# Vision block, prologue and early steps re-ordered, late query/key products in two banks

## The reference

```python
x = layernorm(patches, ln1_g, ln1_b)              # 768 wide
x = layernorm(x @ W + bias, ln2_g, ln2_b) + pe     # 256 wide
h = concat(cls_token + cls_pos, x)                 # 37 tokens
h = h + attention(layernorm(h))                    # 16 heads of 16, rotary on q and k
h = h + ffn(layernorm(h))                          # 256-1024-256, ternary weights, 8-bit tokens
```

## Time and profile before

| | us |
|---|---|
| median of 3 runs | 382.64 (382.4 to 383.99) |
| the profiled execution, its own time | 384.33 |
| its span, first to last instruction | 382.5 |
| TensorE busy | 324.6 |
| VectorE busy | 280.2 |
| ScalarE busy | 217.6 |
| GpSimd busy | 163.5 |

### The profile page before, as it was taken

One profiled execution on the slowest core, in us unless ns is written; L12 is line 12 of the kernel. 1 busy time (PEld: TensorE's weight loads), 2 busy tenths in 40 slices (PEclk: granted clock), 3 DMA queues, 4 the chain that ended last, 5 costly groups with the idle time before them and its releaser, 6 DMA issues.

```text
span 382.5 us, 9772 instructions
## 1 busy us (share of the span) xinstructions
PE 324.6 (85%) x3540; PEld 253.6 (66%) x3548; DVE 280.2 (73%) x683; ACT 217.6 (57%) x395; POOL 163.5 (43%) x330
## 2 busy tenths in 40 slices
PE   1868889999999676899898989889887798999874
PEld 1657777777764332798787878788775476777553
DVE  3599766776856436268967677776766999999983
ACT  2356556575443211435455554646453799999993
POOL 2276534655535436244523233232204456556630
PEclk9999999999999999559999999999999999999997
DMA  8996600000000000000000000000000001000101
GB/s 237 354 402 190 215 3 0 1 2 0 0 3 0 0 0 2 2 2 3 2 1 0 0 0 0 0 0 0 0 2 0 1 2 39 32 27 30 44 28 62
DMA packets 9018, 16.10 MB, mean 42 GB/s; under 512 B 944, under 2 KB 5744, under 8 KB 8992
## 3 DMA queue, kind: packets, MB, share of 16 engines
q1 hardware_dynamic: 7936, 13.59, 10.4%
q10 hardware_dynamic: 1056, 2.18, 1.8%
HBM read 13.34 MB, written 2.42 MB: 41 GB/s over the span
## 4 chain that ended last, share of the span: by engine, by line
PE 49%; DVE 19%; ACT 13%; issue 12%; POOL 4%; DMA 3%; ACTq 0%; DVEq 0%; POOLq 0%
PE ps L333 11%; PE ps L426 10%; DVE sc L837 6%; PE ps L363 5%; DVE ximg L856 4%; PE ps L458 4%; POOL qr L1091 3%; PE ps L434 3%; PE ps L323 3%; ACT ximg L1049 3%; DMA qkT<-in_W 3%; PE ps L445 2%; ACT ximg L1002 2%; PE ps L420 2%; ACT ximg L1044 2%
## 5 line engine op out<-in xcount | busy, mean ns | idle before, releaser
L1083 POOL TENSOR_TENSOR rs<-rs,nhalf 128x1 f32<-128x1 f32 (+1 forms) x76 | 41.2, 548 | 104.9 <-DVE rs L831 43.5
L988 ACT ACTIVATE ximg<-ps,byp 128x222 f32<-128x222 f32 x64 | 25.0, 442 | 61.0 <-PE ps L466 54.1
L333 PE MATMUL ps<-w_in,xT 128*128 128x256 f32 (+1 forms) x228 | 53.2, 383 | 3.8 <-ACT xT L922 3.8
L1133 POOL TENSOR_TENSOR ximg<-qkT,ones_c 128x148 f32<-128x148 f32 x32 | 17.9, 558 | 77.8 <-PE ps L420 76.6
L426 PE MATMUL ps<-hnT,w_v 128*128 (+1 forms) x256 | 38.9, 300 | 12.8 <-ACT ximg L1002 7.6
L333 PEld LDWEIGHTS ps<-w_in,xT 128*128 128x128 f32 (+1 forms) x228 | 41.3, 187 | 11.3 <-ACT xT L922 5.6
L426 PEld LDWEIGHTS ps<-hnT,w_v 128*128 128x128 f32 x256 | 34.2, 208 | 18.2 <-issue 17.0
L363 PE MATMUL ps<-w_qk,hnT 128*128 128x512 f32 (+1 forms) x76 | 36.5, 602 | 8.0 <-DVE qb L701 8.0
L782 DVE TENSOR_TENSOR ximg<-ps,tab 111x512 f32<-111x512 f32 x32 | 22.1, 690 | 28.1 <-PE ps L445 28.1
L693 DVE TENSOR_TENSOR qa<-ps,tab 128x512 f32<-128x512 f32 (+1 forms) x19 | 13.1, 689 | 30.7 <-PE ps L316 30.7
L1091 POOL TENSOR_TENSOR qr<-qa,qb 128x512 f32<-128x512 f32 (+1 forms) x19 | 24.1, 1266 | 14.5 <-DVE qb L701 14.5
(11 more groups left out here) (108 smaller groups left out, 768.8 us busy)
## 6 DMA issues: line engine op xcount, KB each, us to landing
ximg<-in_x SPq DMA_DIRECT2D x18, 384.0 KB, 14.2
out<-ximg SPq DMA_DIRECT2D x18, 128.0 KB, 1.7
ximg<-in_W SPq DMA_DIRECT2D x2, 1024.0 KB, 6.3
...
qkT<-in_W SPq DMA_DIRECT2D x1, 384.0 KB, 4.5
qkT<-in_W ACTq DMA_DIRECT2D x1, 384.0 KB, 9.6
```

The source lines that it names most:

```text
L333: pe.matmul(dst[0:n, :], xT[t % 2][:, k, 0:n], w_in[:, k, :], start=(k == 0), stop=False)
L988: ins = act.activation(vds[u][:, m, :, :].rearrange("p i (r t) -> p i r t", r=3), src, ACT.Identity, bias=b_v[:, m:m + 1])
L1083: pool.tensor_tensor(rs[u][0:n, i:i + 1], rs[u][0:n, i:i + 1], nhalf[0:n, :], ALU.pow).then_inc(S[done], 1)
```

## The change

- **Loads.** W's two halves get semaphores of their own; the first now follows x tile 0 with nothing of the offset table among the next loads of its queue. The constant table is loaded in two parts, columns up to the position table first, then the position table behind W. The offset table is loaded in two column parts: the four that patches need on ScalarE's queue, 111 rows, the three for q, k and output on SP, behind x tile 2. `wide` is loaded in two parts, 256 columns first. x tile 3 now goes ahead of Wqk.
- **Prologue.** 14 matmuls on a block of ones before TensorE's first wait. ScalarE scales W's second half, VectorE the first, and VectorE does so before tile 1's statistics. The five operations on the offset table are re-ordered. `pixels_out(1)` goes ahead of the second bf16 part. `turn_pixels(2)` goes ahead of the offsets of tiles 0 and 1. The work on the 768 columns moves behind ScalarE's steps 3 and 5 and VectorE's steps 4 and 6.
- **`hot` in pieces** of four images, one ahead of each GpSimd step from 2 to 16; each patch offset from tile 2 on waits for its piece.
- **Steps 3 to 8** on TensorE become `early_step`: turn, product, positions, turn of h.
- **From tile 11 on**, odd query/key products go into bank 7, even ones into bank 5, and each waits for the rotation two tiles back, no longer one.

```diff
+        def qk_bank(t):
+            return 7 if t > NT - LAG + 1 and t % 2 else 5
...
             load_x(0)
-            sp.dma_start(w_raw[:, 0:3, :], w_rows[:, 0:3, :]).then_inc(S["ld_w"], 16)
+            sp.dma_start(w_raw[:, 0:3, :], w_rows[:, 0:3, :]).then_inc(S["ld_w0"], 16)
             load_x(1)
-            sp.dma_start(offs[0:48, :], spread_row(a["offsets"], 7 * D, 48)).then_inc(S["ld_offs"], 16)
             load_x(2)
+            sp.dma_start(offs[:, 4 * D:7 * D], spread_row(a["offsets"][4 * D:7 * D], 3 * D, 128)).then_inc(S["ld_rows"], 16)
+            load_x(3)
             sp.dma_start(w_qk[:], a["Wqk"].rearrange("(k p) n -> p k n", p=128)).then_inc(S["ld_qk"], 16)
-            for t in range(3, NT + 1):
+            for t in range(4, NT + 1):
...
-                if t == 2:
-                    pe.wait_ge(S["hot_done"], 2)
+                if isinstance(t, int) and t >= 2:
+                    pe.wait_ge(S["hot_done"], min(t, 16))
...
             def qk_product(t):
                 pe.wait_ge(S["h_canvas"], t + 1)
-                war(pe, "qk_rot", t, 1)
+                late = t > NT - LAG + 1
+                war(pe, "qk_rot", t, 2 if late else 1)
...
+                if qk_bank(t) == 7:
+                    pe.wait_ge(S["y_mid"], NT)
...
+            def early_step(s):
+                turn_pixels(s)
+                patch_product(s - 1)
+                position_rows(s - 2)
+                turn_h(s - 3)
...
+            pe.wait_ge(S["cset"], 1)
+            for i in range(14):
+                pe.matmul(ps[:, 7, 0:128], onesf[:, :], onesf[:, :], start=True, stop=True)
             pe.wait_ge(S["ld_tab"], 16)
             turn_pixels(0)
             patch_offset()
             patch_product(0)
             turn_pixels(1)
             patch_product(1)
+            turn_pixels(2)
             pe.wait_ge(S["hot_done"], 1)
             pe.wait_ge(S["b_done"], 1)
             product_offset(0)
             product_offset(1)
             position_rows(0)
-            turn_pixels(2)
-            for s in range(3, NT + LAG + 1):
+            for s in range(3, LAG):
+                early_step(s)
+            for s in range(LAG, NT + LAG + 1):
                 patch_step(s)
...
+            pixel_stats(0)
+            pixel_mean(0)
+            pixel_var(0)
+            v.wait_ge(S["ld_w0"], 16)
             v.wait_ge(S["ld_byp"], 16)
-            for k in range(3, KP):
+            for k in range(3):
                 ins = v.tensor_scalar(w_in[:, k, :], w_raw[:, k, :], g1[:, k:k + 1], None, ALU.mult)
             ins.then_inc(S["wg_done"], 1)
-            pixel_stats(2)
+            pixel_stats(1)
+            pixel_mean(1)
+            pixel_var(1)
...
-            patch_step(2)
-            v.wait_ge(S["b_mid"], 2)
-            leave_out(pos_rows[:, qo], bmid[0:K3, qo], 1, bres[0:K3, qo]).then_inc(S["b_done"], 1)
-            for s in range(3, NT + LAG + 1):
+            for s in range(2, NT + LAG + 1):
                 patch_step(s)
+                if s == 4:
+                    v.wait_ge(S["b_hi"], 2)
+                    leave_out(bres[0:K3, qo], bhi[0:K3, qo], 0, qko).then_inc(S["b_res"], 1)
+                if s == 6:
+                    v.wait_ge(S["b_mid"], 2)
+                    leave_out(pos_rows[:, qo], bmid[0:K3, qo], 1, bres[0:K3, qo]).then_inc(S["b_done"], 1)
...
             v.memset(ps[:, 0:4, :], 1.0)
+            v.wait_ge(S["qk_rot"], NT)
             v.memset(ps[:, 7, :], 1.0)
...
-            act.dma_start(tab[:, 0:FTAB], a["table"][:, 0:FTAB]).then_inc(S["ld_tab"], 16)
-            act.dma_start(w_raw[:, 3:6, :], a["W"].rearrange("(k p) n -> p k n", p=128)[:, 3:6, :]).then_inc(S["ld_w"], 16)
-            act.dma_start(offs[48:112, :], spread_row(a["offsets"], 7 * D, 64)).then_inc(S["ld_offs"], 16)
-            act.dma_start(wide[:, :], spread_row(a["rows"], 2 * D + F)).then_inc(S["ld_wide"], 16)
+            act.dma_start(tab[:, 0:pe_o], a["table"][:, 0:pe_o]).then_inc(S["ld_tab"], 16)
+            act.dma_start(w_raw[:, 3:6, :], a["W"].rearrange("(k p) n -> p k n", p=128)[:, 3:6, :]).then_inc(S["ld_w1"], 16)
+            act.dma_start(tab[:, pe_o:FTAB], a["table"][:, pe_o:FTAB]).then_inc(S["ld_pe"], 16)
+            act.dma_start(offs[0:K3, 0:4 * D], spread_row(a["offsets"][0:4 * D], 4 * D, K3)).then_inc(S["ld_offs"], 16)
+            act.dma_start(wide[:, 0:D], spread_row(a["rows"][0:D], D)).then_inc(S["ld_g2"], 16)
             act.dma_start(tab[:, FTAB:NTAB], a["table"][:, FTAB:NTAB]).then_inc(S["ld_rot"], 16)
+            act.dma_start(wide[:, D:2 * D + F], spread_row(a["rows"][D:2 * D + F], D + F)).then_inc(S["ld_wide"], 16)
...
+            pixels_out(1)
             act.wait_ge(S["b_res"], 1)
             act.activation(bmid[0:K3, py], bres[0:K3, py], ACT.Copy).then_inc(S["b_mid"], 1)
-            pixels_out(1)
-            act.activation(bhi[0:K3, qo], qko, ACT.Copy).then_inc(S["b_hi"], 1)
             pixels_normal(2)
-            act.wait_ge(S["b_res"], 2)
-            act.activation(bmid[0:K3, qo], bres[0:K3, qo], ACT.Copy).then_inc(S["b_mid"], 1)
             pixels_out(2)
             for s in range(3, NT + LAG + 3):
                 patch_step(s)
+                if s == 3:
+                    act.wait_ge(S["ld_rows"], 16)
+                    act.activation(bhi[0:K3, qo], qko, ACT.Copy).then_inc(S["b_hi"], 1)
+                if s == 5:
+                    act.wait_ge(S["b_res"], 2)
+                    act.activation(bmid[0:K3, qo], bres[0:K3, qo], ACT.Copy).then_inc(S["b_mid"], 1)
...
-            hot_columns(7, B)
             for s in range(2, NT + LAG + 1):
+                if s <= 16:
+                    hot_columns(4 * s - 1, min(B, 4 * s + 3))
                 patch_step(s)
```

More of the change, by code:

```diff
@@ L181, in vit_block @@
         names = (
-            "apart ld_tab ld_rot ld_w ld_byp ld_offs ld_wide ld_qk ld_v ld_o ld_f1 ld_f2 "
+            "apart ld_tab ld_pe ld_rot ld_w0 ld_w1 ld_byp ld_offs ld_rows ld_g2 ld_wide ld_qk ld_v ld_o ld_f1 ld_f2 "
             "cset crow bmix b_hi b_res b_mid b_done wg_done hot_done "
@@ L246, in vit_block, with ps_qk @@
         ps_hT = ps[:, 4, 0:D].rearrange("p (k c) -> p k c", k=2)
-        ps_qk = ps[:, 5, :]
+        def qk_bank(t):
+            return 7 if t > NT - LAG + 1 and t % 2 else 5
+        def ps_qk(t):
+            return ps[:, qk_bank(t), :]
         ps_qkT = ps[:, 6, :].rearrange("p (k c) -> p k c", k=4)
@@ L305, in patch_offset @@
             def patch_offset():
-                pe.wait_ge(S["ld_w"], 32)
+                pe.wait_ge(S["ld_w0"], 16)
+                pe.wait_ge(S["ld_w1"], 16)
                 pe.wait_ge(S["ld_byp"], 16)
@@ L360, in qk_product @@
                     pe.wait_ge(S["b_done"], 2)
-                n = rows(t)
+                if qk_bank(t) == 7:
+                    pe.wait_ge(S["y_mid"], NT)
+                n, dst = rows(t), ps_qk(t)
                 for k in range(2):
-                    pe.matmul(ps_qk[0:n, :], hnT[:, k, 128 * t:128 * t + n], w_qk[:, k, :], start=(k == 0), stop=False)
-                add_rows(ps_qk[0:n, :], t, QK_ROWS).then_inc(S["qk_ready"], 1)
+                    pe.matmul(dst[0:n, :], hnT[:, k, 128 * t:128 * t + n], w_qk[:, k, :], start=(k == 0), stop=False)
+                add_rows(dst[0:n, :], t, QK_ROWS).then_inc(S["qk_ready"], 1)
             def turn_qk(t):
@@ L568, in _ @@
         def _(v):
-            v.memset(onesf[:, :], 1.0)
+            v.memset(onesf[:, :], 1.0).then_inc(S["cset"], 1)
+            v.memset(nhalf[:, :], -0.5).then_inc(S["cset"], 1)
             v.memset(ones_c[:, :], 1.0)
@@ L652, in _ @@
             qo, py = slice(2 * D, 5 * D), slice(0, 2 * D)
-            for t in range(2):
-                pixel_stats(t)
-                pixel_mean(t)
-                pixel_var(t)
-            v.wait_ge(S["ld_w"], 32)
+            pixel_stats(0)
+            pixel_mean(0)
+            pixel_var(0)
+            v.wait_ge(S["ld_w0"], 16)
             v.wait_ge(S["ld_byp"], 16)
-            for k in range(3, KP):
+            for k in range(3):
                 ins = v.tensor_scalar(w_in[:, k, :], w_raw[:, k, :], g1[:, k:k + 1], None, ALU.mult)
             ins.then_inc(S["wg_done"], 1)
-            pixel_stats(2)
+            pixel_stats(1)
+            pixel_mean(1)
+            pixel_var(1)
             v.wait_ge(S["ld_tab"], 16)
-            v.wait_ge(S["ld_offs"], 32)
+            v.wait_ge(S["ld_pe"], 16)
+            v.wait_ge(S["ld_offs"], 16)
+            v.wait_ge(S["crow"], 1)
+            v.tensor_tensor(bfix, ps[0:K3, 6, 0:D], bfix, ALU.add).then_inc(S["bmix"], 1)
             v.tensor_tensor(cls0, cls0, cls1, ALU.add).then_inc(S["bmix"], 1)
@@ L681, in _ @@
             leave_out(pos_rows[:, py], bmid[0:K3, py], 1, bres[0:K3, py]).then_inc(S["b_done"], 1)
-            v.wait_ge(S["b_hi"], 2)
-            leave_out(bres[0:K3, qo], bhi[0:K3, qo], 0, qko).then_inc(S["b_res"], 1)
             nh = 2 * NH
@@ L699, in rotate_sin @@
```

(13 more changed lines are left out.)

14 lines of the change are left out of this document (7 added, 7 removed).

## The result

The changed kernel takes 392.4 us, median of 4 runs (391.16 to 394.75); the kernel before, on the same chip, 383.31. The ratio is 1.0224 (95%: 1.0136 to 1.0312): **slower by 2.2%**, where 375.3 was forecast and 369.2 to 380.2 given as the range. The change is clearly slower; whether by 2% or by less, the interval leaves open. A time is the median of all executions, while a ratio leaves out those more than 1.5% above the fastest of their kernel. The profiled execution took 392.94, its span is 391.1.

The account below looks back on a forecast made before the run. TensorE, busy 85% of the span, was taken as the bound, with gains possible only in prologue, early steps and tail. 1.8 + 5.5 = 7.3 us off the median of 382.64 gave 375.3, range 369.2 to 380.2.

Parts of the forecast that it names:

- the offset load: Prologue loads: the offset part that patches need lands at 12.8 us, between 12.0 and 13.6.
- The lead of 3.7 us in front: Prologue: tile 0's second norm starts at 20.35 us in place of 24.05.
- if the clock isn't up, it stays 5.29: Prologue, patch offset after the warm-up: at low clock 2.5 us more; the forecast took the faster 2.75.
- the second rival: Prologue: W lands at 11.3, the clock stays low until then, no front lead; 379.5 us, chance 0.12.
- The early steps: TensorE's steps 3 to 8: product 8 starts at 52.3 us, before at 54.11; gain 1.8.
- The loop by way of `position_rows`: Early steps: waits through positions and h put turn(s+2) at least 8.5 us behind turn(s).
- the first rival: Early steps: the loop doesn't bind, each step costs 3.95 us, product 8 at 46.2; 369.2 us, chance 0.14.
- Pieces of `hot`: GpSimd steps up to 16: each gets some 0.4 us more while waiting for VectorE; cost nothing.
- Late products: Query/key tail from tile 11: 2.75 us per tile in place of 3.77; gain 5.5, bounds 4.5 and 6.9.
- The hold by the last h tile: Tail's first two intervals: GpSimd's root and shift ahead of tile 11's addition cost an estimated 1.3 us.
- The fourth rival: Tail: rotations and additions hold each other up, period stays 3.77; 380.8 us, chance 0.08.
- Handover: Start of attention at half clock, four steps of 4.9 us: left so, gain 0, risk both ways.

Follow-up runs that it names:

- e1: The changed kernel with its first offset load of 112 rows in place of 111: 383.14 us, ratio 0.9979 to the kernel before.
- e6: e1 with TensorE's early steps in the order turn, positions, product, turn of h: 379.97 us, ratio 0.9887.
- e5: e1 with TensorE's steps 3 to 8 in the order of the kernel before: 379.95 us, ratio 0.989.
- e4: The kernel before with only the two banks for late query/key products added: 382.88 us, ratio 0.9862.
- e12: e4 with 24 unread products of ones (16, 5 and 3) added at the handover to attention: 378.98 us, ratio 0.9868.
- e9: e6 with tile 3's statistics, root and shift taken early and ScalarE's copy of 768 columns ahead of `pixels_out(2)`: 374.03 us, ratio 0.9729.
- e3: The kernel before with its offset table in one load of 112 rows on ScalarE's queue: 381.11 us, ratio 0.9938.
- e14: e9 with 13 unread products of ones (7, 4 and 2) added at the handover to attention: 371.63 us, ratio 0.9653.

## Why the prediction was wrong

**The step that failed is the offset load.** "I take 12.8, between 12.0 and 13.6" landed at 26.08. The sum took bytes ahead of it in the queue and a rate of the whole chip; the rate of this one load, with another row count than the 48 and 64 of before, was not asked. No rival held it. With that one number changed (e1) the kernel stands at 383.14, still not at 375.3: 9 us of the 17 are this step's. The term was short even for a load with a good row count: with 112 rows it lands 11.6 to 13.5 us after its issue at 2.71, so at 14.3 to 16.2, never at 12.8.

**The lead of 3.7 us in front did not come.** In e1, without the load's fault, the norm is at 23.34 for 20.35. Two terms hold this. W's second half was put at 9.2 and came at 10.9, 9.3 after its issue; over the nine traces with this order of loads it took 7.9 to 10.2, before 9.6, so what the order gains lies within the scatter. And the patch offset took 4.43 for 2.75, since TensorE stood idle for 2.19 and its clock fell again; in the changed kernel ScalarE's loads came on top, and it was 5.21. The step "if the clock isn't up, it stays 5.29" was priced, but not that the clock could come up and be lost in the wait behind. This was the second rival's case, to which 0.12 was given. It is not the case of every execution: in e6, with the same loads, W took 7.9 and the patch offset 2.81, the chain then runs by way of the offset load (at 14.33), and the norm is at 21.48. Over the traces that share a prologue the norm lies at 21.48 to 23.72 (e1, e5, e6) and, in the one of before, at 24.05 to 25.37 (before, e4, e12), so the lead is there, but smaller than 3.7 in most.

**The early steps: right in kind, too small in size.** The loop by way of `position_rows` does bind (e6), and the first rival's steps of 3.95 are not seen. Turns 4 to 8 took 20.3 us in e1 and in the changed kernel, the forecast had 19.75. The miss is at the start: turn(4) was put 7.7 behind the norm and came 9.75 behind it in both. The working went by way of `h_first(0)` alone; turn(3), which the same order puts ahead of product 2, waits for tile 3's statistics, and product 2 starts 5.0 to 5.4 behind the norm where the first rival had 2.15. So product 8 is norm + 34.51, not + 31.95, before + 30.06: the loss of 1.9 that the forecast had, and hid behind the lead of 3.7, was 4.45.

**Pieces of `hot` cost nothing**: the long stage from product 8 to tile 10 is 63.52 for 63.57.

**Late products: right.** 5.7 us gained, forecast 5.5 with 4.5 to 6.9. The timeline of the changed kernel, tiles' starts and the last turn of h:

```profile
142.37 0.33 PE L361 MATMUL ps<-tab,hn 64*128 64x64 f32 x2 [1.33 <-ACT hn L960]
...
143.46 1.88 PE L375 MATMUL ps<-w_qk,hnT 128*128 128x512 f32 x4
...
145.83 1.88 PE L375 MATMUL ps<-w_qk,hnT 128*128 128x512 f32 x4
...
148.78 1.88 PE L375 MATMUL ps<-w_qk,hnT 128*128 128x512 f32 x4
...
151.16 1.88 PE L375 MATMUL ps<-w_qk,hnT 128*128 128x512 f32 x4
...
154.10 1.88 PE L375 MATMUL ps<-w_qk,hnT 128*128 128x512 f32 x4
```

Periods of 2.37, 2.95, 2.38 and 2.94 between tiles 13 and 17, mean 2.66, against 2.75 in the forecast. The hold by the last h tile, an estimated 1.3 us, was 1.7: the first two intervals, from 136.26 to 143.46, take 7.20 for 2 x 2.75. The 1.33 of the first row is the part of it in which TensorE idles, and that it equals the estimate is chance. The fourth rival, no overlap, is out.

**Handover: 0 was nearly right.** The stage from values to the end is 1.2 us shorter, the half-clock stretch 13.7 us long for 20.5; in e1, e4, e6 and e9 it is 20.5 again, in e5 13.7 and in e3 6.8, so one trace of each doesn't tie its length to this change. Its price was read too low: 3.6 by four steps of rows 3, about 5.9 by e9 against e14.

By its own steps, then: forecast -7.3 = front and steps -1.8, tail -5.5. Measured without the load's fault (e1, span against span) -1.7 = front -0.7, steps +4.45, tail -5.65, end +0.25. With the fault +8.6. The -1.7 is of two single traces; by the ratio e1 and before can't be told apart.
